# Second layer of a four-layer attention stack: values as weights for four heads side by side, reciprocals as jobs of their own

## The chip, the cores and the metric

The kernel runs on one core of one Trainium2 chip. The metric is the device time of one execution in microseconds: the median over several runs. A profiled execution (the profile) gives one time of its own; its rows are what is read below. In them PE is TensorE's matmul, PEld its load of weights, DVE is VectorE, ACT is ScalarE, POOL is GpSimd and SP is SyncE.

## The reference

Four attention layers follow each other on 16 sequences of 112 tokens of width 256, each with a context of 375 rows. All is float32. Only the second layer changes here. It has 16 heads of width 16:

```python
def _mha(query, key, value, Wq, bq, Wk, bk, Wv, bv, Wa, ba, mask=None):
    q = (query @ Wq + bq).reshape(Nq, Tq, NUM_HEADS, HEAD_DIM)
    k = (key @ Wk + bk).reshape(Nq, Tk, NUM_HEADS, HEAD_DIM)
    v = (value @ Wv + bv).reshape(Nq, Tk, NUM_HEADS, HEAD_DIM)
    attn = jnp.einsum('bthd,bshd->bhts', q, k) / np.sqrt(HEAD_DIM)
    if mask is not None:
        attn = jnp.where(mask == 0, -jnp.inf, attn)
    score = jax.nn.softmax(attn, axis=-1)
    y = jnp.einsum('bhts,bshd->bthd', score, v).reshape(Nq, Tq, D)
    return y @ Wa + ba
t2 = _mha(tgt, tgt, tgt, ..., tgt_mask)                # "own" heads: 112 keys
x = _layer_norm(tgt + t2, ln1_g, ln1_b)
t2 = _mha(x, memory, memory, ...)                      # "cross" heads: 375 keys
x = _layer_norm(x + t2, ln2_g, ln2_b)
t2 = jax.nn.relu(x @ lin1_W + lin1_b) @ lin2_W + lin2_b
return _layer_norm(x + t2, ln3_g, ln3_b)
```

## The kernel before

Each layer is a function (`layer0` to `layer3`; the second layer of the reference is `layer1`) with one hand-written program for each engine. The order of each engine's work is the order of its program, and semaphores with counts tie the engines together. A turn handles two sequences (PAIR = 2, 224 tokens); the second layer has eight turns, in a hardware loop of seven and a last one written out.

Work is in software pipeline. Own attention of the sequences of turn i+1 runs inside turn i. So there is a stretch of own heads ahead of the first turn, and the last turn has no own heads. A turn of `layer1` on TensorE: products for the context's keys (`ck`), output projection of the own heads (`y`), projections of the next tokens (`k`, `q0`, `q1`, `v0`, `v1`), context values (`cv`), cross queries (`cq0`, `cq1`); then the attention's steps, 32 cross heads first (two sequences of 16 heads, one a step), then eight own items of four heads each; beside the own items, from step OWN = 32 on, `side` puts in the cross output projection (`u0`, `u1`), the norm's transposes (`uT`) and the feed-forward (`f0` to `f3`, `z0`, `z1`).

Step n of `lagged` runs the scores of item n, the transposes of item n-2 (LAG_T) and the values of item n-3 (LAG_V). For a cross head that is, on TensorE: one product 112 x 375 (two instructions in float32, L303), three transposes of the probabilities (L313), and three products of the transposed probabilities as weights with the head's values as 17 streamed columns (L335: six instructions; 16 values and a column of ones that gives the softmax's sum). VectorE takes the negated maximum (L401), ScalarE the exponential from PSUM (L373), VectorE copies the transposed probabilities out of PSUM (L405), and for each four heads takes a reciprocal (L416) and multiplies (L419). For an own item VectorE adds the mask (L392) and takes four maxima (L394), ScalarE does four exponentials (L366) and the copy of the transposes (L377); the values are eight instructions (L331). The outputs lie by token, so four transposes each (`OT`, `cOT`, L782) turn them for the projections.

Queries are spread by a mask over eight heads (`qz`, VectorE, L1806; `qz_own`, GpSimd, L1554), so that a product over all 128 rows gives one head's scores.

PSUM has eight banks: three for scores (0 to 2), two for transposed probabilities (3, 4), three (5 to 7) for a ring `P` of all other products, the outputs of the heads among them. A `Ring` gives its jobs the banks in turn; a job waits until the one that last had its bank has been emptied. Probabilities (`p`) and transposed ones (`pT`) have three slots each (PD).

A class `Columns`, used by the other three layers, already takes values as weights: the output of several heads lies in different partitions of one bank (two heads of 64 in the first and third layer, four of 32 in the fourth), L568 for cross heads and L563 for own items; there the probabilities are scaled by the reciprocals ahead of the transposes.

Of the kernel before, what the change touches and what calls it, by code (L numbers as in the profile page):

```python
# [174 lines left out]
PD = 3  # L175
LAG_T, LAG_V = 2, 3


class Phase:

    def __init__(self, name, grouped, heads, dh, q, k, val, ready, bias=None, batches=tuple(range(PAIR)), val_ready=None, ring=None):
        self.batches, self.val_ready, self.ring, self.steps, self.out = batches, val_ready, ring, None, None
        self.name, self.grouped, self.heads, self.dh = name, grouped, heads, dh
        self.q, self.k, self.val, self.ready, self.bias = q, k, val, ready, bias
        self.groups = heads // G
        self.per_batch = self.groups if grouped else heads
        self.items = len(batches) * self.per_batch
        self.keys, self.tiles = (T, 1) if grouped else (CP, CT)  # L190
        self.by_probs = grouped or bias is not None
        self.scored_by = "dve" if self.by_probs else "act"
        self.turned_by = "act" if self.by_probs else "dve"

    def at(self, k):

        return self.batches[k // self.per_batch], k % self.per_batch

    def job(self, k):

        j, r = self.at(k)
        return f"{self.name}O{j}{r if self.grouped else r // G}"

    def closes(self, k):
        return self.grouped or k % G == G - 1

    def output_jobs(self):
        return [(f"{self.name}O{j}{g}", "dve") for j in self.batches for g in range(self.groups)]
# [9 lines left out]
class Attention:  # L218
    def __init__(self, ctx, nc, layer, phases, scored, turned, P):
        self.phases, self.P, self.lag_v = phases, P, LAG_V  # L220
        self.owner = [(ph, k) for ph in phases for k in range(ph.items)]
        n = len(self.owner)
        self.S = Ring(ctx, nc, layer + "_scores", scored, [(m, ph.scored_by) for m, (ph, _) in enumerate(self.owner)])
# [13 lines left out]
        def sb(name, *shape):  # L237
            return ctx.enter_context(nc.sbuf_tensor(f"{layer}_{name}", list(shape), F32))
# [35 lines left out]
    def pass_over(self, eng, name, ph):  # L274

        if name == "pe":
            eng.sem_inc(self.S.full.sem, ph.items)
            eng.sem_inc(self.TR.full.sem, ph.items)
            if not ph.grouped:
                eng.sem_inc(self.values.sem, ph.items // G * (G - 1))  # L280
# [3035 lines left out]
```

## Time and profile before

| | us |
|---|---|
| median of 3 runs | 3822.63 |
| lowest and highest | 3817.73 and 3865.86 |
| the profiled execution, time | 3822.77 |
| its span, first to last instruction | 3821.0 |
| TensorE busy in the span | 3584.9 |
| VectorE busy | 2020.9 |
| ScalarE busy | 1746.1 |
| mean granted TensorE clock | 0.963 |

The granted clock is given as a share of full speed; 1.00 and 0.50 are its levels in this profile. A duration in a row of TensorE runs to the end of the last instruction's way through the array, so rows overlap: what work costs is read from the start of one row to the start of the next. A row that ends in brackets names the idle time ahead of it and what ended it.

### The profile page before, as it was taken

To read this page: it belongs to the slowest core of one execution; us is meant where nothing else is said; L and a number is where in the kernel's file an instruction comes from. 1 tells how busy PE (TensorE), PEld (TensorE's weight loads), DVE (VectorE), ACT (ScalarE), POOL (GpSimd) and SP (SyncE) were. 2 spreads that over 40 slices of the span, in tenths; PEclk is the share of its full clock that TensorE was granted. 3 is DMA by queue.
4 is the path that set the end of the run, shared out by engine and by line. 5 is a ranking of instruction groups with operands and counts; after the bars stand their busy time and mean duration, and the time that the engine had idled before them with its cause. 6 is when DMAs were issued, how large, how long until landed. Compare 5 with 4: busy or idle time off the path is not lost. (4 is left out here: it accounts for less than half of the span.)

```text
span 3821.0 us, 67697 instructions
## 1 busy us (share of the span) xinstructions
PE 3584.9 (94%) x21748; PEld 2729.5 (71%) x21748; DVE 2020.9 (53%) x6215; ACT 1746.1 (46%) x4893; POOL 402.0 (11%) x488
## 2 busy tenths in 40 slices
PE   8999999999989999999997999999999997888888
PEld 6778778887867888888775666666676674565565
DVE  4644555464445555556554445445445445657656
ACT  3544545454443333334333545555555453344444
POOL 2101101110101111101101000000000001211111
PEclk9999999999999999999998999999999998898999
DMA  5000000000040000000001000000000000000000
GB/s 199 4 11 14 9 9 12 14 4 12 6 134 12 13 13 13 7 6 13 13 3 49 8 15 8 8 14 8 8 14 8 8 10 14 11 26 13 13 26 5
DMA packets 58462, 75.11 MB, mean 20 GB/s; under 512 B 6752, under 2 KB 55584, under 8 KB 57024
## 3 DMA queue, kind: packets, MB, share of 16 engines
q1 hardware_dynamic: 58176, 71.45, 5.9%
q8 instruction: 160, 2.62, 0.3%
q14 instruction: 126, 1.03, 0.1%
HBM read 64.04 MB, written 7.40 MB: 19 GB/s over the span
## 5 line engine op out<-in xcount | busy, mean ns | idle before, releaser
L161 PE MATMUL l_bank<-l_xT,weights_of_layers_and 128*128 128x224 f32 x2816 | 619.5, 374 | 17.2 <-ACT l_xT L1161 8.0
L161 PEld LDWEIGHTS l_bank<-l_xT,weights_of_layers_and 128*128 128x128 f32 x2816 | 550.1, 201 | 54.0 <-ACT l_xT L1161 8.7
L614 ACT ACTIVATE l_pT<-l_bank 125x336 f32<-125x336 f32 (+2 forms) x736 | 347.1, 472 | 341.0 <-PE l_bank L546 330.3
L546 PEld LDWEIGHTS l_bank<-identity,l_p 112*125 112x125 f32 (+2 forms) x2336 | 334.8, 178 | 184.6 <-issue 96.8
L546 PE MATMUL l_bank<-identity,l_p 112*125 112x112 f32 (+2 forms) x2336 | 390.0, 279 | 21.6 <-DVE l_p L590 18.2
L631 ACT ACTIVATE l_p<-l_p,l_nm 112x375 f32<-112x375 f32 x384 | 233.4, 608 | 284.9 <-DVE l_nm L665 283.8
L161 PE MATMUL l_bank<-l_cT,weights_of_layers_and 128*128 128x375 f32 x832 | 306.3, 495 | 4.7 <-DVE l_z L1811 3.7
L161 PE MATMUL l_bank<-weights_of_layers_and,l_cT 128*125 128x256 f32 (+2 forms) x960 | 301.0, 451 | 0.2
L728 POOL TENSOR_TENSOR l_ve<-l_mv,eps 112x2 f32<-112x2 f32 (+1 forms) x89 | 17.3, 195 | 2548.7 <-DVE l_mv L722 2548.7
L590 DVE TENSOR_SCALAR l_p<-l_p,l_rs 112x375 f32<-112x375 f32 (+1 forms) x608 | 255.1, 420 | 21.7
L568 PEld LDWEIGHTS l_bank<-l_pT,l_cv 125*64 125x64 f32 (+1 forms) x3648 | 163.6, 131 | 138.7 <-issue 98.7
L627 ACT ACTIVATE l_p<-l_p,l_nm 112x112 f32<-112x112 f32 x512 | 192.2, 377 | 148.6 <-DVE l_nm L661 134.1
L373 ACT ACTIVATE l_p<-l_bank,l_nm 112x375 f32<-112x375 f32 x256 | 145.8, 573 | 247.2 <-DVE l_nm L401 247.2
L665 DVE CUSTOM_DVE_ANT_0 l_p<-l_bank,weights_of_layers_and 112x375 f32<-112x375 f32 x256 | 139.1, 544 | 202.6 <-issue 122.1
L161 PEld LDWEIGHTS l_bank<-l_cT,weights_of_layers_and 128*128 128x128 f32 x832 | 155.4, 195 | 105.6 <-issue 17.9
L568 PE MATMUL l_bank<-l_pT,l_cv 125*64 125x112 f32 (+2 forms) x3648 | 226.0, 273 | 2.0 <-ACT l_pT L614 1.8
L303 PE MATMUL l_bank<-l_ckT,l_qz 128*112 128x375 f32 x512 | 216.9, 510 | 4.5 <-DVE l_qz L1806 3.9
L161 PEld LDWEIGHTS l_bank<-weights_of_layers_and,l_cT 128*125 128x125 f32 x960 | 161.1, 189 | 80.5 <-issue 52.4
L313 PEld LDWEIGHTS l_bank<-identity,l_p 112*125 112x125 f32 (+1 forms) x1024 | 154.4, 179 | 76.0 <-ACT l_p L373 11.2
L538 PE MATMUL l_bank<-l_ckT,l_qz 128*112 128x375 f32 x512 | 203.2, 480 | 0.2
L401 DVE TENSOR_REDUCE l_nm<-l_bank 112x1 f32<-112x375 f32 x256 | 139.1, 546 | 99.4 <-PE l_bank L303 97.7
L538 PE MATMUL l_bank<-l_ckz,l_qT 128*128 128x375 f32 x448 | 177.0, 480 | 0.0
(253 smaller groups left out, 6118.6 us busy)
## 6 DMA issues: line engine op xcount, KB each, us to landing
l_cT<-in_ctx_turned SPq DMA_DIRECT2D x32, 375.0 KB, 3.4
l_cx<-in_ctx SPq DMA_DIRECT2D x16, 375.0 KB
context_rows<-in_ctx_reversed SPq DMA_DIRECT2D x16, 375.0 KB
tokens<-x_after_layer SPq DMA_DIRECT2D x25, 224.0 KB, 2.6
x_after_layer<-l_z SPq DMA_DIRECT2D x24, 224.0 KB, 2.4
weights_of_layers_and<-bias_lines_kept SPq DMA_DIRECT2D x1, 2625.0 KB, 16.3
weights_of_layers_and<-in_L_xattn_w_fused SPq DMA_DIRECT2D x1, 2048.0 KB, 10.7
weights_of_layers_and<-in_L_xattn_w_ff SPq DMA_DIRECT2D x1, 2048.0 KB, 12.7
```

Of the source, the lines that this page charges most:

```text
L161: last = pe.matmul(out, left, right, start=(k == 0), stop=(k == len(pairs) - 1))
L303: last = pe.matmul(bank[:T, 0:S2], ph.q(j, r), ph.k(j, r), start=True, stop=True)
L313: last = pe.transpose(bank[:ph.keys, g * T:(g + 1) * T], p[:, m % PD, g * ph.keys:(g + 1) * ph.keys], ident[:T, :T])
L373: act.activation(p[:, m % PD, 0:S2], S.bank(m)[:T, 0:S2], ACT.Exp, bias=nm[:, ph.col0 + k:ph.col0 + k + 1]).then_inc(S.emptier(m).sem, 1)
L401: dve.tensor_reduce(nm[:, ph.col0 + k:ph.col0 + k + 1], S.bank(m)[:T, 0:S2], AX.X, ALU.max, negate=True).then_inc(self.neg_max.sem, 1)
L538: last = pe.matmul(S.bank(m)[:ph.rows, g * width:(g + 1) * width], ph.q(k, g), ph.k(k, g), start=True, stop=True)
L546: last = pe.transpose(TR.bank(m)[:ph.keys, g * ph.rows:(g + 1) * ph.rows], p[:ph.rows, m % self.p_slots, g * ph.keys:(g + 1) * ph.keys], i ...
L568: last = pe.matmul(bank[a * ph.dh:(a + 1) * ph.dh, column:column + w], ph.val(n, 0, t), pT[:ph.keys, (ph.first + n) % self.pT_slots, t * w ...
L590: eng.tensor_scalar(own, own, self.rs[:r, c:c + 1], None, ALU.mult).then_inc(self.scaled["dve"].sem, 1)
L614: return act.activation(out, src, ACT.Copy)
L627: last = act.activation(own, own, ACT.Exp, bias=nm[:r, c + g:c + g + 1], accum_out=sums[:r, c + g:c + g + 1])
L631: act.activation(own, own, ACT.Exp, bias=nm[:r, c:c + 1], scale=-1.0, accum_out=sums[:r, c:c + 1]).then_inc(self.probs.sem, 1)
```

## The change

Only `layer1` changes; its attention moves from `Attention` and `Phase` (both lose their bodies) to a new class `Quarters` with `Part`.

- Values are the weights. `v` and `cv` are laid out in pairs of heads with 16 zero columns between (48 columns a pair), so that 32 columns hold one head's values and zeros for its neighbour. Four heads, at output partitions 0, 32, 64 and 96, are multiplied one after the other in a burst; the neighbours' burst adds into the same partitions. Eight heads fill 128 partitions, and the result has the turned form that the projection needs: the transposes `OT` and `cOT` go.
- For cross heads a burst follows each fourth step and has 24 instructions; for an own item it is eight.
- The sums of the softmax come from the exponential's accumulator (cross) and a VectorE sum over the probabilities (own). When the heads of a sequence are done, VectorE takes one reciprocal, spreads it over 256 columns, TensorE turns it by two transposes (jobs `cR0`, `cR1`, `sR0`, `sR1` in ring `P`), ScalarE copies it to `OT`, and VectorE multiplies the output with it.
- Lags are 3 for transposes and 4 for values; `p` has 4 slots and `pT` 6. The copy of a cross head's transposes is ScalarE's for even and VectorE's for odd heads.
- Banks: three for scores and two for transposes as before, one (5) for outputs (ring `O`), two (6, 7) for ring `P`.
- The spread cross queries and the feed-forward's hidden values share one array. `v` and `cv` are cleared as a whole at the layer's start.
- In step OWN + 3 nothing is left beside; the cross projection at OWN + 4 waits for the output of each sequence.

```diff
+class Quarters(Attention):
...
+        def values(ph, k):
+            if not ph.bursts(k):
+                return
+            m = ph.first + k
+            job, column, half = ph.place(k)
+            together = [k] * 4 if ph.grouped else list(range(k - 3, k + 1))
+            ready = [TR.got(ph.first + n) for n in together] + ph.val_ready(k)
+            for sem, count in O.free(i, job, *ready) if ph.opens(k) else counts(i, *ready):
+                pe.wait_ge(sem, count)
+            for t in range(ph.tiles):
+                for a, n in enumerate(together):
+                    at = a if ph.grouped else t
+                    last = pe.matmul(O.bank(job)[32 * a:32 * a + 32, column:column + T], ph.val(n, a, t),
+                                     pT[:ph.keys, (ph.first + n) % self.pT_slots, at * T:(at + 1) * T],
+                                     start=(t == 0 and half == 0), stop=(t == ph.tiles - 1 and half == 1))
+            if ph.closes(k):
+                last.then_inc(O.full.sem, 1)
+            else:
+                last.then_inc(self.values.sem, 1)
...
+        self.lagged(parts, [(self.lag_t, turns), (0, scores), (self.lag_v, values)], between)
+
+    def turn_inverses(self, pe, i, P, job, d, ident):
+
+        for sem, count in P.free(i, job, self.spread_out.this(2 * d + 1)):
+            pe.wait_ge(sem, count)
+        for t in range(KT):
+            last = pe.transpose(P.bank(job)[:, t * T:(t + 1) * T], self.spread[:, t * 8:(t + 1) * 8, :].rearrange("p h e -> p (h e)"), ident[:T, :T])
+        last.then_inc(P.full.sem, 1)
...
+                act.activation(slot[:, 0:S2], S.bank(m)[:T, 0:S2], ACT.Exp, bias=nm[:, n, k:k + 1], accum_out=sums[:, n, j, h:h + 1]).then_inc(S.emptier(m).sem, 1)
...
+        self.lagged(parts, [(0, amid), (self.lag_t, turned), (0, exps)], between, amid)
...
+        def totals(ph, k):
+            m, n = ph.first + k, self.phases.index(ph)
+            j, h = ph.head(k, 0)
+            if ph.grouped:
+                dve.wait_ge(self.probs.sem, self.probs.count(i, ph.probs0 + k))
+                own = sums[:, n, j, h:h + 8].rearrange("p (a b) -> p a b", b=2)[:, :, 0] if h % 2 == 0 else sums[:, n, j, h - 1:h + 7].rearrange("p (a b) -> p a b", b=2)[:, :, 1]
+                dve.tensor_reduce(own, p[:, m % self.p_slots, :].rearrange("p (g t) -> p g t", g=G), AX.X, ALU.add).then_inc(self.summed.sem, 1)
+            if ph.closes(k):
+                if ph.grouped:
+                    dve.wait_ge(self.summed.sem, self.summed.count(i, ph.summed0 + k))
+                else:
+                    dve.wait_ge(S.emptier(m).sem, S.count_emptied(i, m))
+                d = ph.job0 + j
+                dve.reciprocal(sums[:, n, j, :], sums[:, n, j, :]).then_inc(self.spread_out.sem, 1)
+                dve.wait_ge(self.spread_out.sem, self.spread_out.count(i, 2 * d))
+                dve.tensor_copy(self.spread[:, :, :], wide(sums[:, n, j, :], 2, 16)).then_inc(self.spread_out.sem, 1)
+
+        def turned(ph, k):
+            if ph.turned_by(k) == "dve":
+                self.turned_copy(dve, i, ph, k, lambda out, src: dve.tensor_copy(out, src))
+
+        def outputs(ph, k):
+            if ph.closes(k):
+                job = ph.place(k)[0]
+                dve.wait_ge(O.full.sem, O.count_full(i, job))
+                sem, count = ph.laid(i, k)
+                dve.wait_ge(sem, count)
+                dve.tensor_tensor(ph.out(k), O.bank(job)[:, 0:TP].rearrange("p (t x) -> p t x", t=KT), ph.out(k), ALU.mult).then_inc(O.emptier(job).sem, 1)
+
+        self.lagged(parts, [(self.lag_t, turned), (0, maxima), (0, amid), (1, totals), (self.lag_v, outputs)], between, amid)
...
-        qz, qz_own = sb("qz", 128, KT, HEADS_PER_TILE, TP), sb("qz_own", 128, KT, HEADS_PER_TILE, TP)
-        v, cv = sb("v", T, PAIR, H, DH + 1), sb("cv", CP, PAIR, CT, H, DH + 1)
+        shared = sb("queries_or_hidden", 128, KT * HEADS_PER_TILE * TP)
+        qz, qz_own = shared[:, :].rearrange("p (k h t) -> p k h t", k=KT, h=HEADS_PER_TILE), sb("qz_own", 128, KT, HEADS_PER_TILE, TP)
+        v, cv = sb("v", T, PAIR, H // 2, 3 * DH), sb("cv", CP, PAIR, CT, H // 2, 3 * DH)
...
-        shared = sb("value_rows_or_hidden", 128, 8 * TP)
-        hid = shared[:, :].rearrange("p (f t) -> p f t", f=8)
+        hid = shared[:, 0:8 * TP].rearrange("p (f t) -> p f t", f=8)
...
+        def value(a, h):
+            return a[:, h // 2, h % 2 * DH:h % 2 * DH + 2 * DH]
+
+        def place(job, n):
+            return job, n // 2 * T, n % 2
...
+                   bias=lambda k: wide(masked[:, :], 1, G), grouped=True, sides=4, turned_by=lambda k: "act")
...
+                     sides=4, turned_by=lambda k: "dve" if k % 2 else "act")
...
-        beside = {OWN + 3: [("cOT", "act")], OWN + 4: [("u0", "dve"), ("u1", "dve")], OWN + 7: [("uT", "act")],
-                  OWN + 8: [("f0", "act"), ("f1", "act")], OWN + 9: [("f2", "act")], OWN + 10: [("f3", "act"), ("z0", "dve"), ("z1", "dve")]}
-
-        before_x = ["ck00", "ck01", "OT", "ck10", "ck11", "y0", "y1"]
-        before_own = ["yT", "cv10", "cq0", "cq1", "cv11"] + [job for job, _ in cross.output_jobs()]
-
-        def names(s):
-            return [job for job, _ in beside.get(s, [])]
-
-        def own_job(s):
-            return [(own.job(s - OWN - LAG_V), "dve")] if s >= OWN + LAG_V else []
-
-        P = Ring(ctx, nc, "l1_product", banks[5:8],
-                 [("ck00", "act"), ("ck01", "act"), ("OT", "act"), ("ck10", "act"), ("ck11", "act"), ("y0", "dve"), ("y1", "dve"),
+        ENDS = OWN + own.items + LAG_VALUES
+        beside = {18: [("cR0", "act")], OWN + 2: [("cR1", "act")], OWN + 4: [("u0", "dve"), ("u1", "dve")], OWN + 6: [("sR0", "act")], OWN + 7: [("uT", "act")],
+                  OWN + 8: [("f0", "act"), ("f1", "act")], OWN + 9: [("f2", "act")], OWN + 10: [("sR1", "act"), ("f3", "act"), ("z0", "dve"), ("z1", "dve")]}
+
+        before_x = ["ck00", "ck01", "ck10", "ck11", "y0", "y1"]
+        before_own = ["yT", "cv10", "cq0", "cq1", "cv11", "cR0"]
+
+        def names(s, own_too=True):
+            return [job for job, _ in beside.get(s, []) if own_too or job[0] != "s"]
+
+        def own_inverses(s):
+            return [job for job in names(s) if job[0] == "s"]
+
+        P = Ring(ctx, nc, "l1_product", banks[6:8],
+                 [("ck00", "act"), ("ck01", "act"), ("ck10", "act"), ("ck11", "act"), ("y0", "dve"), ("y1", "dve"),
...
-        A = Attention(ctx, nc, "l1", [cross, own], banks[0:3], banks[3:5], P)
+                 + [job for s in range(ENDS) for job in beside.get(s, [])])
+        O = Ring(ctx, nc, "l1_output", banks[5:6], cross.output_jobs() + own.output_jobs())
+        A = Quarters(ctx, nc, "l1", [cross, own], banks[0:3], banks[3:5], O, 3, LAG_VALUES, 4, 6)
...
-            for a in (v[:, :, :, DH:], cv[:, :, :, :, DH:]):
-                pool.memset(a, 1.0).then_inc(zeroed, 1)
-            pool.memset(z[:, :, :], 0.0).then_inc(zeroed, 1)
+            for a in (z[:, :, :], v[:, :, :, :], cv[:, :, :, :, :]):
+                pool.memset(a, 0.0).then_inc(zeroed, 1)
...
-                if s == OWN + 3:
-                    turn_tokens(pe, c, P, i, "cOT", A.O, P.got(cross.output_jobs()[-1][0]))
-                elif s == OWN + 4:
-                    attend(i, "u", V["ca"], "cOT")
+            def side(i, s, coming):
+                for d, job in enumerate(("cR0", "cR1", "sR0", "sR1")):
+                    if job in names(s, coming):
+                        A.turn_inverses(pe, i, P, job, d, c.ident)
+                    elif job in names(s):
+                        P.pass_over(pe, "pe", i, [job])
+                if s == OWN + 4:
+                    attend(i, "u", V["ca"], lambda j: O.got(f"cO{j}"))
...
-                turn_tokens(pe, c, P, i, "OT", own.out, P.got_before(own.output_jobs()[-1][0]))
...
-                    last = act.activation(cv[:, j, m, :, 0:DH], P.bank(name)[:CP, a * D:(a + 1) * D].rearrange("p (h d) -> p h d", h=H), ACT.Copy)
+                    last = act.activation(apart(cv[:, j, m]), P.bank(name)[:CP, a * D:(a + 1) * D].rearrange("p (n b d) -> p n b d", b=2, d=DH), ACT.Copy)
...
+            def inverses(i, job):
+                j = int(job[2])
+                act.wait_ge(P.full.sem, P.count_full(i, job))
+                act.activation(OT[:, :, j * T:(j + 1) * T], P.bank(job)[:, 0:TP].rearrange("p (t x) -> p t x", t=KT), ACT.Copy).then_inc(P.emptier(job).sem, 1)
...
+            act.wait_ge(zeroed, 4)
```

## Rows read from the trace of the kernel before

**Rows 1.** Windows, busy us (instructions) by engine, granted clock: second layer, one turn.

```profile
1105.00:2036.50 931.50, 869.01 (x5480) 736.71 (x5480) 487.43 (x1197) 352.83 (x809) 104.06 (x96) 0.94 0.07 23
...
1377.55:1490.01 112.46, 107.84 (x684) 92.04 (x685) 60.15 (x147) 43.92 (x101) 12.74 (x11) 0.94 0.04 11
```

**Rows 2.** TensorE's timeline (start, us, line), steady part of the cross heads.

```profile
1404.70 0.86 PE L303 MATMUL l_bank<-l_ckT,l_qz 128*112 128x375 f32 x2
1405.40 0.48 PE L313 MATMUL l_bank<-identity,l_p 112*125 112x112 f32 x3
1405.72 0.67 PE L335 MATMUL l_bank<-l_cv,l_pT 125*112 125x17 f32 x6
1406.24 0.86 PE L303 MATMUL l_bank<-l_ckT,l_qz 128*112 128x375 f32 x2
```

**Rows 3.** TensorE's waits, then windows as in 1: cross, own, feed-forward, the low clock.

```profile
1453.84 0.93 PE L331 MATMUL l_bank<-l_v,l_pT 112*112 112x17 f32 x8 [1.00 <-ACT l_pT L377]
...
1463.44 1.44 PE L331 MATMUL l_bank<-l_v,l_pT 112*112 112x17 f32 x8 [1.43 <-ACT l_pT L377]
...
1397.80:1446.20 48.40, 47.29 (x328) 38.23 (x328) 35.68 (x86) 17.65 (x31) 1.37 (x3) 1.00 0.08 25
1446.20:1471.36 25.16, 22.73 (x183) 22.04 (x183) 16.65 (x42) 14.39 (x42) 2.17 (x3) 0.85 0.00 0
1471.36:1490.01 18.65, 18.14 (x85) 15.90 (x86) 2.06 (x8) 3.57 (x9) 0.00 (x0) 0.84 0.00 0
1463.40:1477.10 13.70, 13.65 (x59) 13.14 (x60) 4.04 (x12) 5.12 (x14) 1.28 (x1) 0.51 0.00 0
```

**Rows 4.** TensorE's timeline of the third layer, then of the fourth (cross heads there).

```profile
2450.98 0.80 PE L568 MATMUL l_bank<-l_pT,l_cv 125*64 125x112 f32 x12
2451.71 0.58 PE L546 MATMUL l_bank<-identity,l_p 112*125 112x112 f32 x3
2452.12 0.80 PE L538 MATMUL l_bank<-l_ckT,l_qz 128*112 128x375 f32 x2
2452.76 0.48 PE L546 MATMUL l_bank<-identity,l_p 112*125 112x112 f32 x3
...
3336.92 0.80 PE L538 MATMUL l_bank<-l_ckT,weights_of_layers_and 128*112 128x375 f32 x2
3337.65 0.78 PE L568 MATMUL l_bank<-l_pT,l_cv 125*32 125x112 f32 x24
3338.36 1.13 PE L161 MATMUL l_bank<-weights_of_layers_and,l_cT 128*125 128x256 f32 x4
```

**Rows 5.** Groups by line and form (busy us, mean ns, idle before): second, then fourth layer.

```profile
L373 ACT ACTIVATE l_p<-l_bank,l_nm 112x375 f32<-112x375 f32 x256 | 145.8, 573 | 247.2 <-DVE l_nm L401 247.2
L401 DVE TENSOR_REDUCE l_nm<-l_bank 112x1 f32<-112x375 f32 x256 | 139.1, 546 | 99.4 <-PE l_bank L303 97.7
...
L394 DVE TENSOR_REDUCE l_nm<-l_p 112x4 f32<-112x448 f32 x58 | 36.0, 620 | 2.0
...
L1806 DVE SCALAR_TENSOR_TENSOR l_qz<-l_bank,columns,l_headmask 128x1792 f32<-128x1792 f32 x16 | 32.6, 2079 | 46.9 <-PE l_bank L161 46.9
...
L416 DVE RECIPROCAL l_rs<-l_bank 112x4 f32<-112x4 f32 x125 | 21.9, 176 | 97.4 <-PE l_bank L331 93.9 <-PEq L122 3.5
...
L419 DVE TENSOR_TENSOR l_O<-l_bank,l_rs 112x64 f32<-112x64 f32 x64 | 14.4, 224 | 2.2
...
L614 ACT ACTIVATE l_pT<-l_bank 125x336 f32<-125x336 f32 x128 | 56.4, 441 | 54.0 <-PE l_bank L546 53.7
...
L631 ACT ACTIVATION_READ_ACCUMULATOR l_p<-l_p,l_nm 112x1 f32 x128 | 23.9, 187 | 0.0
```

**Rows 6.** TensorE's timeline at the start of a turn's cross part.

```profile
1397.80 2.14 PE L303 MATMUL l_bank<-l_ckT,l_qz 128*112 128x375 f32 x6 [0.56 <-DVE l_qz L1806]
1400.93 0.58 PE L313 MATMUL l_bank<-identity,l_p 112*125 112x112 f32 x3 [0.98 <-ACT l_p L373]
```

**Rows 7.** GpSimd's timeline at the layer's start.

```profile
1105.75 0.27 POOL L1585 MEMSET l_cv<- 125x96 f32 x1
1105.86 0.58 POOL L1586 MEMSET l_z<- 112x512 f32 x1
```

More of the change, by code:

```diff
@@ L170, in wide @@
     return ap.to_broadcast(shape)
[L175 to L208, printed above, removed]
 class Scratch:
@@ L423, in signals @@
-    def signals(self):
-        return [self.neg_max, self.probs, self.values]
 class Part:
@@ L1453, in layer1, with cross_head, own_head @@
         banks = [ctx.enter_context(nc.psum_tensor(f"l1_bank{b}", [128, 512], F32)) for b in range(8)]
+        LAG_VALUES = 4
+        def cross_head(k, g):
+            n = k % H
+            return k // H, n // 8 * 8 + n % 4 * 2 + n % 8 // 4
+        def own_head(k, g):
+            n = k % (H // G)
+            return k // (H // G), n // 2 * 8 + g * 2 + n % 2
         def own_ready(k):
-            return [P.got("k"), q_spread.this(k // 2)] if k < own.groups and k % 2 == 0 else []
+            return [P.got("k"), q_spread.this(k // 2)] if k in (0, 2) else []
@@ L1631, in attend @@
                 for j in range(PAIR):
-                    for sem, count in P.free(i, f"{name}{j}", P.got(turned)):
+                    for sem, count in P.free(i, f"{name}{j}", turned(j)):
                         pe.wait_ge(sem, count)
@@ L1835, in output_norm, with inverses, side @@
                     z_steps.end()
-            def side(i, s):
+            def inverses(i, job):
+                j = int(job[2])
+                dve.wait_ge(P.full.sem, P.count_full(i, job))
+                dve.tensor_copy(OT[:, :, j * T:(j + 1) * T], P.bank(job)[:, 0:TP].rearrange("p (t x) -> p t x", t=KT)).then_inc(P.emptier(job).sem, 1)
+            def side(i, s, coming):
+                for job, e in beside.get(s, []):
+                    if e == "dve" and job[1] == "R":
+                        if job in names(s, coming):
+                            inverses(i, job)
+                        else:
+                            P.pass_over(dve, "dve", i, [job])
                 if s == OWN + 4:
@@ L1903, in _ @@
                 dve.wait_ge(folding, n + 1)
-                dve.tensor_tensor(rows[name][:, :], banks[3 + n][:, 0:D], rows[name][:, :], ALU.add).then_inc(folded, 1)
-            dve.wait_ge(folded, 2)
-            own_steps.start(-1)
-            A.vector(dve, -1, [own], lambda s: P.pass_over(dve, "dve", -1, names(OWN + s)) if names(OWN + s) else None)
-            own_steps.end()
+                dve.tensor_tensor(rows[name][:, :], banks[3 + n][:, 0:D], rows[name][:, :], ALU.add).then_inc(prepared, 1)
+            dve.wait_ge(prepared, FOLDED)
+            A.vector(dve, -1, [own], first_side)
             with dve.Fori(0, TURNS - 1) as i:
```

433 lines of the change are left out of this document (202 added, 231 removed).

## The prediction

> **What bounds the kernel now.** I read the table of stages first. The second layer holds 931.5 of 3821.0 us, with TensorE busy for 869.0, VectorE for 487.4 and ScalarE for 352.8; one middle turn of it takes 112.46 us [rows 1]. TensorE sets the pace, so I then read its timeline in the steady part of the cross scores. There a head repeats every 1.54 us without an idle line: 0.70 from the scores to the transposes, 0.32 to the values, 0.52 to the next scores [rows 2]. Six instructions of 17 columns cost nearly as much as the two of 375 columns: each waits for its own 112-column weights. Last I read the stretch of the own heads. From its first scores to the feed-forward are 25.16 us, and 18.65 from there to the next turn, 43.8 together; inside lie waits of 1.00 and 1.43 us for a copy of ScalarE, and right behind the second a piece of 13.7 us at a granted clock of 0.51 [rows 3]. That is the lower of the clock's two levels (1.2 in place of 2.4 GHz); it costs about half of itself, 6.8 us a turn. Six of the seven full turns take between 110.8 and 112.5 us, by what this piece holds; one of them stands in [rows 1], and its row is the upper end.
>
> The sum is made against the profiled execution, 3821.0 us of span and 3822.8 with what lies around it, 0.2 above the median of the runs (3822.63). A change of 2% (76 us) is what I call distinguishable here.
>
> **Values of the cross heads.** The change turns the product around: four heads are 24 instructions with 32-column weights, each head on its own quarter of the output partitions, 112 columns streamed. The fourth layer runs just this shape: its 24 instructions take 0.71 us until the next starts, and the scores ahead of them 0.73 in place of the 0.63 that they take ahead of anything else; transposes behind a burst (the third layer's, of 12) take 0.41 in place of 0.32 [rows 2, 4]. A burst so costs 0.71 + 0.10 + 0.10 = 0.91 us. The scores themselves are the same two instructions, 0.63, and the transposes 0.32. Four heads: 4 x 0.95 + 0.91 = 4.71 in place of 4 x 1.54 = 6.16, 1.178 a head, 0.36 less.
>
> The Trainium skill says that changing the tiling mode drains TensorE (TensorEngine Tiling, Key Properties). The two tenths found in [rows 4] agree; were the drain free, four heads would be 4.51, and the layer 13 us faster still.
>
> Whether the others keep up at 1.18: VectorE has a maximum of 0.55 and, for odd heads only, a copy, which I price as ScalarE's 0.44: 0.77 a head. ScalarE has the exponential of 0.57, the reading of its sum (new here, 0.19) and half a copy of 0.44, 0.98 a head [rows 5]. Both are under 1.18. The chain decides with the rings: the transposes of a head, three steps behind its scores, need the copy of the head two before, and that copy stands on ScalarE behind this head's exponential. Scores 0.80, maximum 0.55, exponential 0.57, reading 0.19 (0.10 of it not hidden, my choice), copy 0.44 and some 0.2 of signals are 2.7, with the 0.32 ahead of the scores 3.0 for three steps. Three steps with a burst are 3.8, three without 2.85: a stall of 0.15 in one head of four, 0.04 a head. The third score bank stays, and the scores need their bank only after 2.2 of 2.85. With VectorE's output norm in the first seven steps (three pieces of some 0.9) I take 1.5 us of stalls a turn. From the first transposes to the first own scores the turn before has 1400.93 to 1446.20, 45.3 us [rows 3, 6]; after, 29 steps of 0.95 and seven bursts, 27.6 + 6.4 = 33.9, and 1.5: **9.9 less a turn**.
>
> **Own heads.** Each item gets 8 instructions in four quarters, a third of the burst of 24: 0.24 plus the two switches, 0.45, where the 8 had 0.72 (bounds: 0.24, and 0.72 for no gain). But VectorE gets work. In the 25.16 us it was busy 16.65. It loses six reciprocals with their products (0.18 + 0.22 each, 2.4) and a copy (0.4). It gets eight sums over 112x448, priced as the maximum of that shape, 0.62 (5.0), three closings of a reciprocal and a spreading copy (0.58 each, 1.7), and two products of 0.4 [rows 3, 5]: 21.4. The 0.4 for copy and product is an estimate for 224 to 256 columns, between the rows of 64 (0.22) and 448 (0.62). TensorE's own work in these eight steps is 15 to 16 us. So here VectorE becomes the bound. I went through the steps in each engine's order: the product that empties the output bank (there is one) stands behind the sum, and this behind four exponentials. The first own values then wait about 2.1 us for it. The transposes of the normed tokens wait 1.9 for the norm, the fifth item's values 1.35 for the bank. The feed-forward begins 21.4 us after the stretch's start, the turn ends 15.4 later: 36.8 at full clock. Before it was 43.8 - 6.8 = 37.0. TensorE waits longer than before, 5.4 against 2.4 us, so the low clock will not go. A drop at the first of these waits costs 7.2 (the stretch is then TensorE's again and the feed-forward begins at 26), one at the last only 3. I take 6: 42.8, **1.0 less a turn**.
>
> **Two banks for the products in place of three.** Each product now waits for the emptying of the one before the last. Going through the turn's start with 0.84 us from a bank's last instruction to its release (0.27 and the copy), I find waits of 0.3, 0.25, 0.25 and 0.1. The last context values wait for the bank that VectorE's spreading of the queries holds for 2.08 us [rows 5]: 1.4 idle, where 0.56 stood [rows 6]. The scores begin 0.9 later. But the first maximum waits for the second spreading anyway, and the exponential for that, as the wait of 0.98 shows [rows 6]: it absorbs all but **0.2 a turn**. The four transposes of own outputs and the four of cross outputs go, eight of the reciprocals come: equal, in the shadow of other waits. The queries in the feed-forward's room add no wait, since their readers are done 8 steps before it is written, and the other way round.
>
> **Start.** The values' arrays are now cleared as a whole ahead of the first TensorE instruction. From 512 columns at 0.58 and 96 at 0.27 follow some 0.75 ns a column: 768 and 2304 columns add **2.4 us**, once [rows 7]. The stretch of own heads ahead of the first turn I leave at nothing: its VectorE work grows, its waits for copies shrink with the deeper lag; bounds -3 and +3.
>
> **Sum.** Seven full turns: 7 x (-9.9 - 1.0 + 0.2) = -75. The last turn has the cross part alone, and its values of three heads (1.5) become part of a burst: -9.9 and -1.5, -11.4. Start +2.4. Together -84: 3822.8 - 84 = **3739 us**.
>
> **The rivals.**
> (a) The low clock goes, or comes where TensorE waits anyway: 6 x 7 = 42 less, 3697. For it: the piece begins right behind the one wait of 1.43 us, and a lag deeper by one step could take this one away. Against it: TensorE waits longer than before. 0.16.
> (b) A second piece of low clock each turn, at the start of the cross part, where 1.4 us of waiting come: 13.7 us of bound work at half, 6.8 x 8 = 54 more, 3793. For it: 1.43 us sufficed in the own stretch. Against it: 0.56 and 0.98 within 3.1 us did not [rows 6]. 0.12.
> (c) The chain of maximum, exponential, reading and copy holds the cross step. From rows it is 3.0 us for three steps; it decides from 3.6 on, and at 4.2 the step is 1.40 in place of 1.21: 0.19 x 256 = 49 more, 3788. Against it: the third layer's rows, with the same order of steps, stand without a wait [rows 4]. 0.11. The Trainium skill warns of this: with TensorE four times faster, emptying PSUM may become the bottleneck, and both ScalarE and VectorE should do it (TensorEngine Tiling, PSUM Bottleneck). The change splits the copies of the cross heads and leaves all those of the own ones to ScalarE.
> (d) The other side: the waits keep the clock low from the own heads to the end of the feed-forward. TensorE's 31.4 us of work there become 62.8, 20 more than my 42.8, x 7 = 140: 3879, slower. It decides from a piece of 13.7 + 2 x 12 = 38 us a turn on. Against it: before, the clock came back within 6 us of the feed-forward's start [rows 3], and the feed-forward has no waits. 0.05.
> (e) The four quarters don't overlap in this kernel: 24 instructions of 0.1 and the switches are 2.6 in place of 0.91, 0.42 x 256 = 108 more, 3847. [rows 4] speak against it. 0.02.
>
> **How the numbers follow.** The forecast has 0.54; its own range is 3715 to 3765 (the drop's 3 to 7.2 a turn, stalls of 0.5 to 3 a turn, the start's bounds). Eight times in ten: from (a) to (b), 3697 to 3793. Faster by over 2% means under 3746: all of (a) and 0.38 of the forecast's 0.54, 0.54. Slower: (d), 0.05. Within 2%: the rest, 0.41.
>
> **What would show it.** TensorE's timeline in the cross part: heads of 0.95 and each fourth with a burst of 24 lasting 0.7; 1.25 or more on average speaks for (c). In the own stretch VectorE is busy for over 20 us without a pause and the releasers of TensorE's waits are VectorE's product and norm; the turn takes about 101.4 us. The granted clock by pieces decides (a), (b) and (d). Wrong most easily: how long the low clock lasts, for which I have a bound and no rule.

## The result and the profile after

| | before | after |
|---|---|---|
| median of the runs, us | 3826.02 (4 runs) | 3713.93 (4 runs) |
| lowest and highest | 3817.73 and 3865.86 | 3713.08 and 3717.15 |
| span of the profiled execution | 3821.0 | 3711.6 |
| mean granted TensorE clock | 0.963 | 0.968 |

After to before is 0.969, 95% interval 0.962 to 0.976. The forecast was 3739, with 3697 to 3793 around it: 25 us more came off than forecast. The kernel before has single runs near 3870 among those near 3822, so the experiments below are compared with the changed kernel, which repeats within 5 us.

Windows of the changed kernel (busy us and instructions of PE, PEld, DVE, ACT, POOL, then granted clock, DMA share, GB/s), answering [rows 1, 3]: the second layer, one turn, its own heads, its feed-forward, the low clock in it.

```profile
1105.00:1927.00 822.00, 743.18 (x5480) 545.63 (x5480) 453.04 (x971) 415.30 (x1209) 106.51 (x96) 0.95 0.08 26
1368.36:1467.17 98.81, 91.63 (x685) 67.29 (x685) 55.67 (x120) 51.69 (x151) 12.74 (x11) 0.97 0.04 12
1407.10:1428.01 20.91, 15.66 (x176) 13.00 (x174) 19.32 (x43) 13.46 (x44) 2.17 (x3) 0.95 0.00 0
1428.01:1445.93 17.92, 17.92 (x98) 14.97 (x99) 1.37 (x5) 4.63 (x12) 0.00 (x0) 0.86 0.00 0
1426.00:1432.90 6.90, 5.70 (x24) 4.63 (x22) 2.27 (x6) 2.86 (x8) 0.45 (x1) 0.51 0.00 0
```

All of the gain lies in this layer: 822.0 for 931.5 us, 109.5 less, against 109.4 of the span. TensorE runs the same 5480 instructions and is busy 126 us less. The own heads take 20.91 us, and VectorE is busy for 19.32 of them, TensorE for 15.66. The piece of low clock is half as long as in [rows 3].

TensorE's timeline in the cross heads, answering [rows 2]: one round of four heads, from a burst to the next.

```profile
1396.35 0.78 PE L571 MATMUL l_bank<-l_pT,l_cv 125*32 125x112 f32 x24
1397.06 0.58 PE L556 MATMUL l_bank<-identity,l_p 112*125 112x112 f32 x3
1397.47 0.80 PE L548 MATMUL l_bank<-l_ckT,l_queries_or_hidden 128*112 128x375 f32 x2
1398.11 0.48 PE L556 MATMUL l_bank<-identity,l_p 112*125 112x112 f32 x3
1398.42 0.80 PE L548 MATMUL l_bank<-l_ckT,l_queries_or_hidden 128*112 128x375 f32 x2
1399.06 0.48 PE L556 MATMUL l_bank<-identity,l_p 112*125 112x112 f32 x3
1399.37 0.80 PE L548 MATMUL l_bank<-l_ckT,l_queries_or_hidden 128*112 128x375 f32 x2
1400.02 0.57 PE L556 MATMUL l_bank<-identity,l_p 112*125 112x112 f32 x3
1400.43 0.80 PE L548 MATMUL l_bank<-l_ckT,l_queries_or_hidden 128*112 128x375 f32 x2
1401.16 0.78 PE L571 MATMUL l_bank<-l_pT,l_cv 125*32 125x112 f32 x24
```

Start to start, the round is 4.81 us: transposes to scores 0.41, 0.31, 0.31, 0.41, scores to transposes 0.64, scores to burst 0.73, burst 0.71. No row has a wait in brackets, but one short wait is hidden. These are the same transposes' weight loads (PEld), the third and the fourth of the round, with ScalarE's copy between them:

```profile
1398.74 0.61 PEld L556 LDWEIGHTS l_bank<-identity,l_p 112*125 112x125 f32 x3
...
1399.45 0.44 ACT L617 ACTIVATE l_pT<-l_bank 125x336 f32<-125x336 f32 x1
...
1400.02 0.40 PEld L556 LDWEIGHTS l_bank<-identity,l_p 112*125 112x125 f32 x3 [0.46 <-ACT l_p L613]
```

The third transposes begin at 1399.06, 0.32 after their first load. The fourth begin together with theirs, 0.13 after the end of ScalarE's copy (1399.89), and take 0.41. They need the bank that this copy empties; L613, the name in brackets, had ended 0.47 before. So ScalarE's chain costs 0.10 us in one head of four. Behind a burst the load also begins with the transposes (1397.06, 0.41), whether the last copy ended 0.08 or over 2 us before.

TensorE's waits in the same turn: four of the own heads, then the start of the next turn, answering [rows 3, 6].

```profile
1411.02 0.59 PE L556 MATMUL l_bank<-identity,l_p 112*112 112x112 f32 x4 [0.54 <-ACT l_pT L617]
...
1415.95 0.40 PE L571 MATMUL l_bank<-l_pT,l_v 112*32 112x112 f32 x8 [1.52 <-DVE l_OT L663]
...
1425.23 0.57 PE L758 MATMUL l_bank<-identity,l_x 112*128 112x112 f32 x4 [1.99 <-DVE l_x L1857]
...
1427.34 0.60 PE L571 MATMUL l_bank<-l_pT,l_v 112*32 112x112 f32 x8 [1.12 <-DVE l_OT L663]
...
1467.17 1.13 PE L161 MATMUL l_bank<-weights_of_layers_and,l_cT 128*125 128x256 f32 x4 [1.16 <-DVE l_queries_or_hidden L1839]
1468.13 2.05 PE L548 MATMUL l_bank<-l_ckT,l_queries_or_hidden 128*112 128x375 f32 x6
1470.39 0.58 PE L556 MATMUL l_bank<-identity,l_p 112*125 112x112 f32 x3 [0.20 <-ACT l_p L613]
```

Groups by line and form in the layer, answering [rows 5] (busy us, mean ns, idle before): the own sum, the product that empties the output bank, the spreading copy, VectorE's copy, ScalarE's reading of the sum.

```profile
L655 DVE COPY l_pT<-l_bank 125x336 f32<-125x336 f32 x128 | 64.3, 502 | 34.1 <-PE l_bank L556 33.6
...
L642 DVE TENSOR_REDUCE l_sums<-l_p 112x4 f32<-112x448 f32 x64 | 39.1, 610 | 3.8 <-ACT l_p L608 3.8
...
L663 DVE TENSOR_TENSOR l_OT<-l_bank,l_OT 128x224 f32<-128x224 f32 x32 | 12.4, 387 | 6.4 <-PE l_bank L571 5.5
...
L651 DVE COPY l_spread<-l_sums 112x256 f32<-112x256 f32 x32 | 9.4, 294 | 1.1
...
L613 ACT ACTIVATION_READ_ACCUMULATOR l_p<-l_bank,l_nm 112x1 f32 x256 | 49.5, 193 | 0.0
```

### The profile page after: what moved, and what is told of

It is laid out like the page before. It is cut to its first block and busy times, and to the rows that moved or that the text cites. A ratio compares the mean times of both kernels' runs of the same rounds, so it can differ in the third digit from the quotient of the medians.

```text
span 3711.6 us, 67721 instructions
## 1 busy us (share of the span) xinstructions
PE 3455.0 (93%) x21748; PEld 2536.0 (68%) x21748; DVE 1990.7 (54%) x5991; ACT 1807.5 (49%) x5293; POOL 404.1 (11%) x488
## 5 line engine op out<-in xcount | busy, mean ns | idle before, releaser
L161 PE MATMUL l_bank<-weights_of_layers_and,l_cT 128*125 128x256 f32 (+2 forms) x960 | 303.3, 454 | 11.4 <-DVE l_queries_or_hidden L1839 9.3
L311 PE MATMUL l_bank<-l_ckT,l_qz 128*112 128x375 f32 x512 | 203.2, 481 | 0.2
L548 PE MATMUL l_bank<-l_ckT,l_queries_or_hidden 128*112 128x375 f32 x512 | 201.2, 479 | 0.0
L556 PEld LDWEIGHTS l_bank<-identity,l_p 112*125 112x125 f32 (+1 forms) x1024 | 139.8, 174 | 83.7 <-ACT l_p L613 27.7
L613 ACT ACTIVATE l_p<-l_bank,l_nm 112x375 f32<-112x375 f32 x256 | 146.6, 573 | 91.2 <-DVE l_nm L634 89.2
L556 PE MATMUL l_bank<-identity,l_p 112*125 112x112 f32 (+1 forms) x1024 | 170.2, 279 | 7.5 <-ACT l_pT L617 5.3
```

What stands on the lines that cost most here:

```text
L161: last = pe.matmul(out, left, right, start=(k == 0), stop=(k == len(pairs) - 1))
L311: last = pe.matmul(S.bank(m)[:ph.rows, g * width:(g + 1) * width], ph.q(k, g), ph.k(k, g), start=True, stop=True)
L548: last = pe.matmul(S.bank(m)[:T, g * width:(g + 1) * width], ph.q(k, g), ph.k(k, g), start=True, stop=True)
L556: last = pe.transpose(TR.bank(m)[:ph.keys, g * T:(g + 1) * T], p[:, m % self.p_slots, g * ph.keys:(g + 1) * ph.keys], ident[:T, :T])
L613: act.activation(slot[:, 0:S2], S.bank(m)[:T, 0:S2], ACT.Exp, bias=nm[:, n, k:k + 1], accum_out=sums[:, n, j, h:h + 1]).then_inc(S.emptier ...
```

## The experiments

Where no count of runs is given, a time below is that of a single run. One cut of a middle turn is used throughout, read off TensorE's timeline (for the kernel before, as in [rows 3]): cross (first cross scores to first own scores), own (to the feed-forward's first product), feed-forward (to the next turn's first product), start (to the next cross scores).

| kernel | cross | own | feed-forward | start | median, us |
|---|---|---|---|---|---|
| before | 48.40 | 25.16 | 18.65 | 20.25 | 3826.02 |
| after | 37.77 | 20.91 | 17.92 | 22.20 | 3713.93 |
| bursts head by head | 42.29 | 20.90 | 16.99 | 22.20 | 3744.75 |
| before, deeper lags alone | 47.38 | 25.89 | 17.22 | 20.24 | 3830.32 |
| after, lags of before | 43.24 | 24.03 | 16.72 | 22.10 | 3784.39 |
| output before sum | 37.77 | 20.89 | 17.92 | 22.20 | 3716.89 |
| 2 score, 2 output banks | 40.56 | 20.90 | 18.44 | 22.20 | 3735.43 |
| 2 score, 3 product banks | 41.53 | 21.01 | 17.00 | 19.85 | 3726.96 |
| own sums on ScalarE | 37.78 | 19.67 | 17.06 | 22.20 | 3698.59 |
| the same, copy on VectorE | 37.77 | 18.38 | 17.18 | 22.20 | 3687.23 |

**The order inside a burst.** Rival (e): do the four quarters overlap, and is it the order round the quarters that makes them? The two loops change places.

```diff
-            for t in range(ph.tiles):
-                for a, n in enumerate(together):
+            for a, n in enumerate(together):
+                for t in range(ph.tiles):
```

> The changed kernel, but the 24 instructions of a burst of cross heads go head by head (six to the same quarter of the output partitions, then the next quarter) in place of round the four quarters. The work and the banks are the same. Theory (the gain of the cross heads is the four quarters running at the same time): a burst grows from 0.71 us towards 24 x 0.1 = 2.4 us, some overlap may stay where one head follows the other; 64 bursts by 0.7 to 1.7 are 45 to 109 us more, 3760 to 3823. Rival (streaming turned round, or the smaller weights, is the gain, and the order doesn't matter): 3714 within 0.3%.

Measured: 3744.75 us, 31 more. TensorE's timeline, a burst and what follows:

```profile
1385.31 1.43 PE L571 MATMUL l_bank<-l_pT,l_cv 125*32 125x112 f32 x24
1386.67 0.58 PE L556 MATMUL l_bank<-identity,l_p 112*125 112x112 f32 x3
```

The burst lasts 1.36 us in place of 0.71. Seven of a turn's eight bursts lie in the cross part, which grows by 4.52 us, about 7 x 0.65. The eighth lies in the own heads, which stay at 20.90: TensorE's wait for VectorE's product there falls from 1.52 to 0.87 us. Over seven full turns the cross parts add 31.6, the feed-forwards give 6.3 back (the low clock behind the own heads lasts 3.4 us in place of 6.8), and the last turn adds 5.4: 31 in all. So the quarters work side by side when neighbours in the order lie in different quarters. One thing the run does not separate: head by head, neighbours in the order also add into the same sums. The Trainium skill says that different tiles can load weights and multiply in parallel (TensorEngine Tiling, Key Properties); both traces agree. The time lies below the 3760 to 3823 that I expected: head by head, the 24 instructions still cost less than the 2.08 us of the 24 before (4 x 0.52, [rows 2]), one burst a turn is hidden, and the low clock got shorter.

**The lags alone.** The kernel before with lags 3 and 4, four slots of `p` and `pT`, the work beside the own heads one step later, and the queries in the feed-forward's room.

```diff
-PD = 3
-LAG_T, LAG_V = 2, 3
+PD = 4
+LAG_T, LAG_V = 3, 4
...
```

> The kernel before, with the deeper lags alone: transposes 3 and values 4 steps behind the scores, four slots for probabilities and transposed ones, the side work of the own stretch one step later (and the queries in the feed-forward's room, for the space). No values as weights, no new banks. Theory (bursts bring most, lags little): the waits of 1.00 and 1.43 us a turn for ScalarE's copy go, with them perhaps the low clock that follows, 6.8 a turn: between 2 and 9 us a turn, 3760 to 3809. Rival (the lags did most of it): under 3760. If 3815 or more, the lags are worth nothing without the rest.

Measured: 3830.32 us. TensorE's waits in the layer (total us, times, longest), of this kernel:

```profile
PE l_bank L331 <- ACT l_pT L377: 23.7, 21, 1.4
PE l_bank L303 <- ACT l_p L373: 7.8, 8, 1.0
```

The 1.4 for ScalarE's copy stays, with one step more of distance. In the class of before, the exponentials of a step stand ahead of the copy in ScalarE's order, so the deeper lag moves the copy's reader and its writer together. My belief that the lag would take this wait away fell. The seven full turns take 777.9 us for 778.6, and the layer's first cross scores come 3.8 later, behind 27 us at half clock from 1133.4 on. The lags alone are worth nothing in the order of before. In the changed kernel ScalarE makes the copy ahead of the exponentials of its step; no run changes this order alone, so its share stays open.

**The changed kernel with the lags of before.** The other way round.

```diff
-        LAG_VALUES = 4
+        LAG_VALUES = 3
-        A = Quarters(ctx, nc, "l1", [cross, own], banks[0:3], banks[3:5], O, 3, LAG_VALUES, 4, 6)
+        A = Quarters(ctx, nc, "l1", [cross, own], banks[0:3], banks[3:5], O, 2, LAG_VALUES, 4, 6)
```

> The changed kernel with the old lags of 2 and 3 steps; all else stays. Theory (the chain of scores, maximum, exponential with its reading, transposes must fit into the lag): 0.8 + 0.55 + 0.57 + 0.1 + signals and the 0.32 ahead of the scores are some 2.5 us, where two steps without a burst are 1.9: the cross step grows from 1.2 to 1.25 to 1.35 us, 13 to 38 us more over 256 heads, and the own stretch gets waits for ScalarE's copy: 3727 to 3765. Rival (TensorE's own work bounds the cross part at any lag): 3714 to 3720.

Measured: 3784.39 us, 70 more, beyond my range. TensorE's waits in the layer:

```profile
PE l_bank L556 <- ACT l_p L613: 38.1, 80, 1.1
PE l_bank L571 <- ACT l_pT L617: 24.4, 15, 2.2
PE l_bank L556 <- ACT l_p L608: 17.2, 17, 1.3
```

Now the chain of maximum, exponential and accumulator sets the cross step (+5.5 a turn) and ScalarE the own heads (+3.1). With steps of 0.95 in place of 1.54 us, two steps no longer hold the 2.2 us of scores, maximum, exponential and reading. The lags have no worth alone, and 70 of the 112 us gained hang on them. The clock is not the reason: it was low for 6.8 us behind the own heads in six of the seven turns here too.

**The product ahead of the sum.** VectorE's order in the own heads is changed, so that the output bank is emptied ahead of the sum of the next item.

```diff
-(0, amid), (1, totals), (self.lag_v, outputs)], between, amid)
+(0, amid), (self.lag_v, outputs), (1, totals)], between, amid)
```

> The changed kernel, but in each step VectorE does the product that empties the output bank ahead of the sum over the probabilities of the step before. Theory (the first own values wait because this product is queued behind the sum, and the sum behind four exponentials): the wait of 1.5 us a turn shrinks by 0.6 to 0.9 and the one of 1.15 by up to 0.5, the wait for the norm (2.0) stays: 0.6 to 1.4 a turn, 3703 to 3710. Rival (the product is late because VectorE as a whole is late; the order is worth nothing, time comes back as a longer wait for the norm): 3711 to 3716.

Measured: 3716.89 us, no gain. TensorE's waits in the layer:

```profile
PE l_bank L758 <- DVE l_x L1857: 20.5, 9, 4.6
...
PE l_bank L571 <- DVE l_OT L663: 11.4, 14, 1.1
...
PE l_bank L161 <- ACT l_xT L1737: 4.8, 8, 0.6
```

The wait for the product fell from 19.9 to 11.4, and those for the norm and what follows it grew; the stretch is 20.89 for 20.91. That is the rival's account. An order shifts the wait; VectorE's sum of work stays.

**Where the third score bank goes.** Two score banks, and the third given to the outputs, then to the products.

```diff
-        O = Ring(ctx, nc, "l1_output", banks[5:6], cross.output_jobs() + own.output_jobs())
+        O = Ring(ctx, nc, "l1_output", [banks[5], banks[2]], cross.output_jobs() + own.output_jobs())
-        A = Quarters(ctx, nc, "l1", [cross, own], banks[0:3], banks[3:5], O, 3, LAG_VALUES, 4, 6)
+        A = Quarters(ctx, nc, "l1", [cross, own], banks[0:2], banks[3:5], O, 3, LAG_VALUES, 4, 6)
```

> The changed kernel with the third score bank given to the outputs: two banks for scores, two for outputs. Theory: the waits for the one output bank (1.5 and 1.15 a turn) go, 18 us; but the scores then need the bank of the head two before, 2.2 us after its scores (0.8 + 0.55 + 0.57 + 0.1 + signals), where two steps without a burst are 1.9 us: up to 0.3 us in three of four heads, 7 us a turn, 55 more: 3730 to 3755. Rival (two score banks are enough because a burst in every fourth step gives the time back): 3690 to 3700.

```diff
-        P = Ring(ctx, nc, "l1_product", banks[6:8],
+        P = Ring(ctx, nc, "l1_product", [banks[6], banks[7], banks[2]],
...
-        A = Quarters(ctx, nc, "l1", [cross, own], banks[0:3], banks[3:5], O, 3, LAG_VALUES, 4, 6)
+        A = Quarters(ctx, nc, "l1", [cross, own], banks[0:2], banks[3:5], O, 3, LAG_VALUES, 4, 6)
```

> The changed kernel with the third score bank given back to the ring of products: two for scores, three for products. Theory: the wait of 1.16 us for the spread queries and the small waits at the turn's start go but were absorbed (0.2 a turn, 1 to 2 us in all); the scores' price is that of the run with two score banks and two output banks: together 3745 to 3770, and the difference to that run is the worth of the second output bank, about 18 us. Rival (the two-bank ring costs real time): at most 5 us over that run.

Measured: 3735.43 and 3726.96 us. TensorE's timeline at the start of a turn, with three product banks:

```profile
1370.44 1.51 PE L548 MATMUL l_bank<-l_ckT,l_queries_or_hidden 128*112 128x375 f32 x4 [0.56 <-DVE l_queries_or_hidden L1839]
1373.66 0.88 PE L548 MATMUL l_bank<-l_ckT,l_queries_or_hidden 128*112 128x375 f32 x2 [1.71 <-ACT l_p L613]
```

The third score bank is worth 2.8 us of cross part a turn in the one and 3.8 in the other, where the third scores wait 1.71 for it. A third product bank gives 2.35 back at the start (19.85 for 22.20), a second output bank nothing in the own heads (20.90). I had put the product bank's worth at 0.2 a turn and was surprised by 3726.96; the trade goes to the scores, but narrowly. Of the 2.35, 1.0 is lost again in the cross part (41.53 for 40.56), because scores that begin earlier wait longer for their third bank; 1.4 a turn is what the product bank is worth net. With two output banks TensorE's waits for VectorE's product are gone, but those for the norm (20.5 us in the layer) and for ScalarE's copy behind it (10.0 for 0.9) grew in their place, and the stretch stays at 20.90. My 18 us for that bank fell. The feed-forward's 17.00 and 18.44 go with granted clocks of 0.91 and 0.84 there.

**The clearing.** Only the zero columns between the values are cleared.

```diff
-            for a in (z[:, :, :], v[:, :, :, :], cv[:, :, :, :, :]):
+            for a in (z[:, :, :], v[:, :, :, DH:2 * DH], cv[:, :, :, :, DH:2 * DH]):
```

> The changed kernel, but at the layer's start only the 16 zero columns between the two heads of a pair are cleared (256 and 768 columns in place of 768 and 2304); the others are written before they are read. Theory: 2048 columns fewer at 0.75 ns, 1.5 to 2.2 us earlier, once: 3711 to 3713. Rival (the start is hidden behind the loads): unchanged. The difference may be seen only in the trace, in the start of TensorE's first instruction of the layer (1110.98).

Measured: 3715.76 us, the same. TensorE's first row in the layer, with the idle time ahead of it:

```profile
1110.52 1.01 PE L758 MATMUL l_bank<-identity,tokens 112*128 112x112 f32 x4 [8.55 <-DVEq L129]
```

The idle time is 8.55 us here, 10.27 in the changed kernel and 6.90 before: the clearing costs 3.4 and half of it can go, but this is less than the runs scatter.

**The sums on ScalarE.** If VectorE bounds the own heads, taking the eight sums from it must help. The exponential's accumulator gives them.

```diff
-                    last = act.activation(own, own, ACT.Exp, bias=nm[:, n, k * G + g:k * G + g + 1])
+                    j, h = ph.head(k, g)
+                    last = act.activation(own, own, ACT.Exp, bias=nm[:, n, k * G + g:k * G + g + 1], accum_out=sums[:, n, j, h:h + 1])
...
-                dve.tensor_reduce(own, p[:, m % self.p_slots, :].rearrange("p (g t) -> p g t", g=G), AX.X, ALU.add).then_inc(self.summed.sem, 1)
```

> The changed kernel, but the sums of the own heads come from the exponentials' accumulator on ScalarE (four readings of some 0.1 an item) in place of a VectorE sum of 0.53 to 0.61 an item. Theory (VectorE's occupation bounds the own stretch): VectorE loses 4.2 us of its 21 in the stretch, its product and norm come earlier, TensorE's waits for them (1.5, 2.0, 1.15 a turn) shrink by half or more: 2 to 4 us a turn, 3685 to 3700. Rival (the waits are latency of the chain, not occupation; or ScalarE takes VectorE's place): 3708 to 3716.

Measured: 3698.59 us. TensorE's waits in the layer:

```profile
PE l_bank L752 <- DVE l_x L1851: 10.5, 9, 4.6
PE l_bank L161 <- ACT l_xT L1731: 9.9, 8, 1.3
...
PE l_bank L553 <- ACT l_pT L615: 7.9, 14, 0.9
PE l_bank L568 <- ACT l_pT L615: 7.2, 19, 0.6
PE l_bank L568 <- DVE l_OT L657: 3.2, 4, 1.3
```

The waits for VectorE's product fell from 19.9 to 3.2 us and for the norm from 19.7 to 10.5; ScalarE's copies took part of their place. The own heads take 19.67; VectorE and ScalarE are now busy 15.88 us each in them. A further step gives the copy of the normed tokens' transposes (`uT`) to VectorE and takes the shorter clearing.

```diff
-OWN + 7: [("uT", "act")]
+OWN + 7: [("uT", "dve")]
+                elif s == OWN + 7:
+                    dve.wait_ge(P.full.sem, P.count_full(i, "uT"))
+                    dve.tensor_copy(xT[:, :, :].rearrange("p a b -> p (a b)"), P.bank("uT")[:, 0:2 * TP]).then_inc(P.emptier("uT").sem, 1)
```

> The changed kernel once more, unaltered, on the same chip as the next two and timed with them: 3711 to 3717 us. It is the yardstick for a gain of less than half a per cent.

> The own heads' sums of exponentials are taken by the exponentials themselves on ScalarE, timed in rounds. In one look this gave 3698.59, 15 us less than 3713.93. If that is the VectorE-bound stretch of the own heads giving way, it stays: 3694 to 3703. If it was the luck of one chip, it comes within 3 us of the unaltered kernel beside it.

> As the run before, and the copy of the transposed x for the feed-forward goes from ScalarE to VectorE, and only the zero columns of the value arrays are cleared. With the sums on ScalarE, TensorE waited 9.9 us in the layer for that copy (l_xT from ScalarE, eight times, up to 1.3 each) and VectorE is no longer the last. If ScalarE's queue is what is late there: 3686 to 3696. If VectorE, which must also make the norm ahead of it, is as late: 3697 to 3705.

Measured, six runs each on one chip: 3715.63 (3712.14 to 3716.43), 3703.75 (3701.07 to 3707.75) and 3687.23 (3675.45 to 3695.32). The second is 12 below the unaltered kernel, so the gain stays, though 3703.75 is 0.8 above the range that I had given it and 5 above the single run. To before (3822.46) the last is 0.9605, interval 0.9545 to 0.9665: it beats both kernels. The sums give 12 us, the copy with the shorter clearing 16 more; no run has that copy alone. Windows of the last kernel, own heads and feed-forward as above:

```profile
1399.84:1418.22 18.38, 15.44 (x176) 12.95 (x175) 16.02 (x36) 14.48 (x70) 2.17 (x3) 1.00 0.00 0
1418.22:1435.40 17.18, 17.18 (x102) 14.41 (x99) 1.19 (x4) 5.58 (x18) 0.00 (x0) 0.90 0.01 1
```

TensorE 15.44, VectorE 16.02 and ScalarE 14.48 busy us in 18.38: the three are now nearly level. The profiled execution is the slowest of the six; its runs spread over 20 us and the mean granted clock goes with them (0.970 at 3695.32, 0.975 at 3675.45). Why, stays open.

## Why the prediction was right, and where its sizes were off

- **Cross heads: right.** Predicted from the first transposes to the first own scores 35.4 us a turn, 9.9 less; measured 1371.59 to 1407.10, 35.5, and 9.8 less by [rows 3, 6]. The price of the burst, taken from the rows of the third and the fourth layer [rows 4], came out to the hundredth: 0.71 us, with a tenth ahead and a tenth behind it. The 1.5 us of stalls came out as a sum, not as I had made it up. The stall of one head in four came, 0.10 where the chain of 3.0 us in 2.85 gave 0.15 (0.6 a turn). For the rest I had named VectorE's output norm; the rows show the reciprocal's transposes (0.2), a wait for ScalarE's copy at the part's start (0.4) and one row of transposes more than I had counted (0.3). The tenth ahead of a burst and the tenth behind it agree with the drain that the Trainium skill names (TensorEngine Tiling, Key Properties).
- **Rival (c) came only as far as that tenth**, because the lag is 3; the run with the lags of before shows it in full, at +5.5 a turn. The Trainium skill's advice that both engines empty PSUM (TensorEngine Tiling, PSUM Bottleneck) agrees with the last two runs: one copy moved from ScalarE to VectorE gave, with the clearing, 16 us.
- **Own heads: right.** Predicted 21.4 us with waits of 2.1, 1.9 and 1.35; measured 20.9 with 1.52, 1.99 and 1.12, the releasers as said. The sum was priced 0.62 and took 0.61, the product 0.4 and took 0.39, reciprocal with copy 0.58 and took 0.54. The work was counted less well than this suggests: I added durations (21.4), but VectorE's rows overlap (a sum of 0.61 is followed after 0.53) and one of the three closings lies outside, so it is busy 19.32 us, with 1.6 of waits, and not for over 20 without a pause; that 21.4 comes near 20.9 is partly luck. That VectorE was the bound is shown by four runs: its order, a second output bank and a longer burst leave the stretch at 20.89 or 20.90, and only taking the sums away shortens it.
- **The low clock: the term that was mis-sized.** I priced 6 us a turn, between 7.2 for a drop at the first wait and 3 for one at the last. It came between the last two waits: six of seven turns have 6.9 us at half clock, from 1426.0, in the row shown (0.51). From 1427.34, where TensorE works again, to 1432.9 that costs half of 5.6, 2.8 a turn. 3.2 too much over seven turns is 22 us, about the 25 that I missed. Own heads and feed-forward so fell from 43.81 to 38.83 us, 5.0 in place of 1.0; over all seven turns the mean fell from 42.9 to 38.8, 4.2. Rival (a), that the low clock goes, did not happen; its number (3697) lies nearer to the 3714 than the forecast's 3739 because half of the piece went. Rivals (b) and (d) did not come.
- **Two banks for the products: too cheap.** Predicted 0.2 a turn. From the turn's first product to the first transposes it was 23.38 and is 24.46 (1445.93 to 1470.39): 1.1. The wait for the spreading bank was seen rightly (1.16 for 1.4); small gaps at the transposes (0.68 from start to start, 0.4 before) add what I had left out. The run with three product banks puts their worth at 1.4 a turn.
- **First own stretch: 6.8 us less** (20.3 for 27.1), where I had 0 with bounds of 3 both ways. There the values waited for ScalarE's copies in before, 1.50 us once and five times 0.2 to 0.6, with nothing else to fill TensorE, and the stretch stood at half clock for 10 us; after, for 7. The clearing at the **start** took 3.4 for 2.4, and the first turn's start 1.9 more than before, as in every turn. **Last turn**: 15.3 for 11.4.

Summed by traces: seven turns -91.6 (on average from 111.2 to 98.1; predicted -75), ahead of the first cross scores -1.5 (+2.4), last turn -15.3 (-11.4): -108.4 us (-84). The smaller misses lie on both sides; the low clock's 22 us carry most of the difference.

## What to carry to other kernels

Price a new form of instruction from a place of the same program where it already runs, with the switch ahead of it and behind it; that price held to a hundredth. Add up an engine's work from start to start, not by the durations of its rows, which overlap. A wait too short for brackets can be seen in the weight loads: a load that is not ahead of its product tells of one. When TensorE's steps get shorter, count again how many of them the chain of the other engines needs, and which engine bounds each stretch: the lag that was worth nothing before was worth 70 us after. When an engine becomes the bound, changing its order moves the wait, and only taking work from it shortens the stretch.

## What the hardware showed that was not expected

- The piece of low clock did not grow with the waits. Before, 1.00 and 1.43 us of waits had 10.2 to 13.7 us at half clock behind them; after, 1.52, 1.99 and 1.12 had 6.9; with the sums on ScalarE it was 3.4 or 6.9, turn about, in turns of 96.7 and 97.8 us. Its place and length can be read in a trace; these runs give no rule to say them ahead.
- 24 products of 112 columns with 32-column weights take 0.71 us round the quarters and 1.36 quarter by quarter.
- The reading of the exponential's accumulator has a row of 0.19 us, the same behind 112 and 375 columns, but the next instruction starts 0.09 behind its start:

```profile
1404.28 0.39 ACT L606 ACTIVATE l_p<-l_p,l_nm 112x112 f32<-112x112 f32 x1 [2.07 <-DVE l_nm L630]
1404.57 0.19 ACT L606 ACTIVATION_READ_ACCUMULATOR l_p<-l_p,l_nm 112x1 f32 x1
1404.66 0.37 ACT L606 ACTIVATE l_p<-l_p,l_nm 112x112 f32<-112x112 f32 x1
```

From the first exponential of this own item to the copy behind the fourth are 1.50 us, 1.14 without the readings. Four readings so hold ScalarE 0.37 us more, and take from VectorE a sum that holds it 0.53: the accumulator is the cheaper way by itself, and it takes the work from the engine that was the bound.
